# Perceiver block on one core: value projection for four heads at 512 columns, streamed value weights, and a reordered start of the tail

## What is computed

```
q = (query @ Wq + bq)            # 32 heads of 128, in 8 groups of 4
k, v = split(kv @ Wkv + bkv)     # 8 key/value heads of 128, kv = the 6272 context rows
scores = q.k / sqrt(128); attn = softmax(scores); o = attn @ v
x = x + o @ Wo + bo
```

## Time and profile before

| | us |
|---|---|
| median of 3 runs (1044.91 to 1045.31) | 1045.17 |
| the profiled execution | 1043.96 |
| its span, from the first to the last instruction | 1042.2 |
| PE busy | 1016.8 (98%) |
| DVE, ACT, POOL busy | 758.4, 590.3, 474.3 |

### The profile page before, as it was taken

How to read it: one execution, slowest core, us unless ns; L and a number is a source line. 1 busy time by engine, 2 the same in 40 slices (tenths; PEclk the granted TensorE clock), 3 DMA queues, 4 the chain that set the end, 5 groups by cost and what they waited for, 6 DMA issues and landing times.

```text
span 1042.2 us, 19683 instructions
## 1 busy us (share of the span) xinstructions
PE 1016.8 (98%) x7083; PEld 933.9 (90%) x7083; DVE 758.4 (73%) x1676; ACT 590.3 (57%) x1249; POOL 474.3 (46%) x637
## 2 busy tenths in 40 slices
PE   7999999999999999999999999999999999999997
PEld 5878989999999999999999999999999999999643
DVE  5777777767877687777876777777877678766665
ACT  5465566556656566555665566565665556655430
POOL 2344544455534545455544455445454444544330
PEclk9999999999999999999999999999999999999999
DMA  9731211122212222122221222112222115353966
GB/s 311 245 126 59 64 55 55 59 65 59 69 41 69 76 63 69 41 69 67 71 57 54 65 60 69 59 56 68 66 63 65 57 42 168 118 152 117 304 201 221
DMA packets 73537, 98.91 MB, mean 95 GB/s; under 512 B 8688, under 2 KB 42496, under 8 KB 73440
## 3 DMA queue, kind: packets, MB, share of 16 engines
q1 hardware_dynamic: 72448, 96.12, 30.1%
q10 hardware_dynamic: 896, 1.51, 0.4%
q0 software_dynamic: 96, 0.02, 0.0%
HBM read 82.81 MB, written 14.81 MB: 94 GB/s over the span
## 4 chain that ended last, share of the span: by engine, by line
PE 86%; DMA 5%; DVE 4%; ACT 2%; POOL 2%; SPq 1%; issue 1%; POOLq 0%; DVEq 0%
PE p_kv L73 18%; PE p_kv L74 18%; PE p_kv L75 18%; PE p_t L670 7%; PE p_o L73 4%; PE p_o L74 4%; PE p_o L75 4%; PE p_s L73 2%; PE p_s L74 2%; PE p_s L75 2%; PE p_s L753 2%; DMA wkv_raw<-in_wkv 1%; PE p_o L680 1%; PE p_ot L658 1%; DMA expanded_weights<-slots 1%; DMA ctx_st<-in_ctx_t 1%
## 5 line engine op out<-in xcount | busy, mean ns | idle before, releaser
L523 POOL TENSOR_SCALAR slots<-code 128x512 f32<-128x512 bf16 x232 | 154.1, 664 | 224.0 <-DVE slots L1296 153.3
L1292 DVE TENSOR_TENSOR slots<-slots 128x512 f32<-128x512 f32 x232 | 176.3, 760 | 3.3 <-POOL slots L523 1.5
L543 POOL TENSOR_TENSOR slots<-slots 128x512 f32<-128x512 f32 x58 | 75.7, 1304 | 202.5 <-DVE slots L1292 202.5
L1101 ACT ACTIVATE slots<-code,drop_and_offsets 128x512 f32<-128x512 bf16 x232 | 148.4, 714 | 29.8 <-POOL slots L543 29.1
L1245 DVE TENSOR_TENSOR v_lo<-p_kv,v_hi 128x256 fp32r<-128x256 f32 x196 | 83.2, 425 | 107.7 <-ACT v_hi L1066 106.6
L1066 ACT ACTIVATE v_hi<-p_kv 128x256 fp32r<-128x256 f32 x196 | 75.1, 384 | 137.8 <-PE p_kv L75 137.2
L1257 DVE TENSOR_TENSOR pt_lo<-p_t,pt_hi 128x512 fp32r<-128x512 f32 x224 | 133.4, 617 | 23.3 <-ACT pt_hi L1077 23.3
L1247 DVE SCALAR_TENSOR_TENSOR k_lo<-p_kv,bk_sb,k_hi 128x448 fp32r<-128x448 f32 x112 | 76.3, 682 | 100.3 <-ACT k_hi L1066 99.6
L1066 ACT ACTIVATE k_hi<-p_kv,bk_sb 128x448 fp32r<-128x448 f32 x112 | 70.9, 634 | 130.7 <-PE p_kv L75 129.8
L1077 ACT ACTIVATE pt_hi<-p_t 128x512 fp32r<-128x512 f32 x224 | 115.0, 542 | 41.6 <-PE p_t L670 41.5
L73 PE MATMUL p_kv<-wkv_hi,ctx_even_hi 128*128 128x256 f32 x448 | 126.4, 282 | 1.0 <-DVE v_lo L1245 0.9
(11 more groups left out here) (238 smaller groups left out, 2694.2 us busy)
## 6 DMA issues: line engine op xcount, KB each, us to landing
code<-in_codes SPq DMA_DIRECT2D x58, 256.0 KB, 2.7
scale<-in_scales SPq DMA_DIRECT2D x116, 128.0 KB, 3.1
expanded_weights<-slots SPq DMA_DIRECT2D x56, 256.0 KB, 2.1
ctx_st<-in_ctx_t SPq DMA_DIRECT2D x96, 112.0 KB, 2.0
ring_hi<-expanded_weights SPq DMA_DIRECT2D x22, 256.0 KB, 5.4
ring_lo<-expanded_weights SPq DMA_DIRECT2D x22, 256.0 KB, 5.3
wq_hi<-in_wq SPq DMA_DIRECT2D x4, 1024.0 KB, 6.5
wq_lo<-in_wq SPq DMA_DIRECT2D x4, 1024.0 KB, 6.5
```

Of the source, the lines that this page charges most:

```text
L523: nc.gpsimd.tensor_scalar(slots[:, slot, :], code16[:], LINES[j][0], LINES[j][1], ALU.mult, ALU.add).then_inc(pool_lines, 1)
L1101: nc.scalar.activation(slots[:, slot, :], code16[:], ACT.Identity, bias=offsets[:, k:k + 1], scale=LINES[j][0]).then_inc(act_lines, 1)
L1292: nc.vector.tensor_tensor(slots[:, slot, :], slots[:, slot, :], slots[:, other, :], ALU.max).then_inc(merged, 1)
```

## The change

- `values` runs only in blocks 0 and 4 of a chunk and projects four heads at once: 7 tiles of 12 matmuls of 512 columns. `v_hi`, `v_lo` hold four heads; splits and roundings have 512 columns.
- The value weights no longer stay. SP loads the 512 columns of the next group (1 MB) into `vw_lo` when the values of this one are done (`load_vw`); ACT and DVE round and split them in two halves of 128x1024, in the two blocks that follow (`round_vw`, `split_vw`). The key weights are loaded in four pieces.
- The NF4 tiles are no longer one to a block: of four tiles n to n+3, three are joined inside the block with the values and the fourth in the fourth block. Merges 0 to 4 of tile n stand ahead of the first split of values; those of n+1 and n+2 stand between the splits, by `between_tiles`. The context pieces are spread as `BLOCK_PIECES`.
- The ring has 18 slots, with a new `AHEAD`; SP's `scales_of(NB + 1)` is gone from its stream, POOL issues that load; the last blocks' attention turns, `fold(0)`, and the sums on DVE change their order.

In the rewritten schedules only the new side is shown, in the order SP, POOL, PE, ACT, DVE.

```diff
-PAIR_PIECES = (5, 5, 5, 1)
+VGROUP = 4
+VCOLS = VGROUP * D
+BLOCK_PIECES = (4, 2, 2, 2, 4, 1, 1, 0)
...
+        vw_hi = sb(st, "vw_hi", [P, KT, VCOLS], F32R)
+        vw_lo = sb(st, "vw_lo", [P, KT, VCOLS], F32R)
+        v_hi = sb(st, "v_hi", [P, CT, VCOLS], F32R)
+        v_lo = sb(st, "v_lo", [P, CT, VCOLS], F32R)
...
-        KV_USES = CT + 4
+        KV_USES = CT + 2 * VGROUP
+        GROUPS = NKV // VGROUP
...
+        RING_PLACES = [("hi", 0), ("lo", 0), ("hi", 1), ("lo", 1), ("hi", 2), ("lo", 2), ("v_hi", 0), ("v_hi", 1),
+                       ("v_lo", 0), ("v_lo", 1), ("hi", 3), ("lo", 3)]
+        WB = RING_ODD + len(RING_PLACES)
...
+            def load_vw(group):
+
+                if group >= 1:
+                    s, h = (group - 1) // GROUPS, (group - 1) % GROUPS * VGROUP
+                    sp.wait_ge(kv_psum, v_use(s, h, CT - 1) + 1)
+                first = NKV * D + group % GROUPS * VCOLS
+                sp.dma_start(vw_raw[:], wkv[:, :, first:first + VCOLS]).then_inc(vw_in, 16)
 
...
+                    if h % VGROUP == 0:
+                        if start:
+                            load_wq(3)
+                        load(0)
+                        codes_of(n + 2)
+                        if start:
+                            load_wq(4)
+                        load(1)
+                        if start:
+                            load_wq(5)
+                        tile_out(n)
+                        scales_of(n + 1)
+                        if start:
+                            load_wkv(2)
+                            load_wq(6)
+                        if last and h == 0:
+                            for dst, src in ((co, coefs), (mk, mask)):
+                                sp.dma_start(dst[:], src).then_inc(coef_in, 16)
                         codes_of(n + 3)
+                        load(2)
+                        tile_out(n + 1)
+                        scales_of(n + 2)
+                        if start:
+                            load_wq(7)
+                        codes_of(n + 4)
+                        load(3)
+                        if GROUPS * s + h // VGROUP + 1 < GROUPS * NCH:
+                            load_vw(GROUPS * s + h // VGROUP + 1)
+                        if start:
+                            load_wkv(3)
+                        tile_out(n + 2)
+                        scales_of(n + 3)
+                        if last:
+                            ring_slots(h)
+                    elif h % VGROUP == 1:
+                        load(0)
+                        codes_of(n + 5)
+                        load(1)
+                        if last:
+                            ring_slots(h)
...
-                if slot == WB + 12:
-                    scales_of(NB + 1)
...
+                    if h % VGROUP == 0:
+                        last_line(n)
+                        narrow(n + 1)
+                        split(0)
+                        join(n)
+                        first_lines(n + 1)
+                        add_rowsum(i, h)
+                        last_line(n + 1)
+                        narrow(n + 2)
+                        split(1)
+                        join(n + 1)
+                        first_lines(n + 2)
+                        last_line(n + 2)
+                        narrow(n + 3)
+                        split(2)
+                        join(n + 2)
+                        first_lines(n + 3)
+                        split(3)
+                    elif h % VGROUP == 1:
+                        last_line(n + 3)
+                        narrow(n + 4)
+                        split(0)
+                        add_rowsum(i, h)
+                        split(1)
+                    elif h % VGROUP == 2:
+                        split(0)
+                        add_rowsum(i, h)
+                        split(1)
+                    else:
+                        split(0)
+                        add_rowsum(i, h)
+                        if last and h == NKV - 1:
+                            wait_apart(pool, rows_in, 16 * len(rows), pool_passed)
+                            nc.gpsimd.tensor_tensor(x_bo[:], x_sb[:], bo_sb[:], ALU.add).then_inc(step("x_bo"), 1)
+                            nc.gpsimd.memset(la[:, :, 5 * RANK:6 * RANK], 0.0).then_inc(step("la_apart"), 1)
+                            nc.gpsimd.tensor_tensor(two_idents[:], ident[:, 0:TOK], ident[:, TOK:P], ALU.add).then_inc(
+                                step("two_idents"), 1)
+                        join(n + 3)
+                        first_lines(n + 4)
+                        split(1)
 
...
+            wait_apart(pool, scaled, NB + 1, pool_passed)
+            for b in range(2):
+                pool.dma_start(scale[b * QBLK:(b + 1) * QBLK, :],
+                               scales[NB + 1, b].partition_broadcast(QBLK)).then_inc(step("last_scale_in"), 16)
...
-                        m = split_matmuls(nc, p_kv[:, v_bank(h, t), 0:2 * D], ctx_hi[half][:, k, keys],
-                                          ctx_lo[half][:, k, keys], wkv_hi[:, k, cols], wkv_lo[:, k, cols],
+                        m = split_matmuls(nc, p_kv[:, v_bank(h, t)], ctx_hi[half][:, k, keys],
+                                          ctx_lo[half][:, k, keys], vw_hi[:, k], vw_lo[:, k],
...
-            prev_values(NCH, 0)
-            turn_attention(5)
-            project_out(5)
-            turn_attention(6)
-            turn_output(NB - 1)
-            project_out(6)
-            turn_attention(7)
-            project_out(7)
-            used[0] += 3 * KT // 2
...
+            turn_attention(5)
+            turn_attention(6)
+            prev_values(NCH, 0)
+            project_out(5, 0)
+            turn_output(NB - 1)
+            project_out(5, 1)
+            project_out(6)
+            turn_attention(7)
...
             pe.wait_ge(step("two_idents"), 1)
             mean_and_turn(0, xa)
...
+            def round_vw(n):
+                act.wait_ge(vw_in, 16 * (n // 2 + 1))
+                nc.scalar.activation(vw_piece(vw_hi, n), vw_piece(vw_raw, n), ACT.Copy).then_inc(vw_rounded, 1)
...
+                if h % VGROUP == 0:
+                    for t in range(CT):
+                        if i == 0 and t in (1, 2, 4, 5):
+                            query_out({1: 2, 2: 3, 4: 4, 5: 5}[t])
                         round_values(s, h, t)
+                        if t == 0:
                             round_ctx(s, h, half, 0, last)
+                        elif t == 1:
+                            lines(n + 1, part=slice(0, 2))
+                        elif t == 2:
+                            lines(n + 1, part=slice(2, 4))
+                        elif t == 3:
+                            round_ctx(s, h, half, 1, last)
+                            if s == 0:
+                                round_wkv(h // 2 + 1)
+                        elif t == 4:
+                            lines(n + 2, part=slice(0, 2))
+                        elif t == 5:
+                            lines(n + 2, part=slice(2, 4))
+                        else:
+                            round_ctx(s, h, half, 2, last)
                     if i == 0:
+                        query_out(6)
...
+                    group = GROUPS * s + h // VGROUP + 1
+                    if h % VGROUP < 3 and group < GROUPS * NCH:
+                        round_vw(2 * group + h % VGROUP - 1)
+                    round_ctx(s, h, half, 0, last)
...
+                if h % VGROUP == 0:
+                    lines(n + 3)
+                elif h % VGROUP == VGROUP - 1:
+                    lines(n + 4)
...
+            def split_vw(n):
+                dve.wait_ge(vw_rounded, n + 1)
+                nc.vector.tensor_tensor(vw_piece(vw_lo, n), vw_piece(vw_raw, n), vw_piece(vw_hi, n).bitcast(F32),
+                                        ALU.subtract).then_inc(vw_split, 1)
...
+                if h % VGROUP == 0:
+                    for k in range(5):
+                        merge(n, k)
+                    between_tiles = {0: ((0, 5),), 1: ((1, 0),), 2: ((1, 1), (1, 2), (1, 3)), 3: ((1, 4), (1, 5)),
+                                     4: ((2, 0),), 5: ((2, 1), (2, 2), (2, 3)), 6: ((2, 4), (2, 5))}
                     for t in range(CT):
+                        if i == 0 and t in (1, 2, 4, 5):
+                            finish_query({1: 1, 2: 2, 4: 3, 5: 4}[t])
+                        split_kv(v_use(s, h, t), v_lo[:, t], p_kv[:, v_bank(h, t)], v_hi[:, t])
+                        for later, k in between_tiles[t]:
+                            merge(n + later, k)
+                        if s == 0 and t == 3:
+                            split_wkv(h // 2 + 1)
+                    if i == 0:
+                        finish_query(5)
                 else:
...
+                    for k in range(2):
+                        merge(n + 3, 2 * (h % VGROUP - 1) + k)
+                    if s == 0 and h == 2:
+                        split_wkv(2)
```

(3 more changed lines are left out.)

300 lines of the change are left out of this document (111 added, 189 removed).

## The result

The changed kernel takes **1076.78 us** (median of 4 runs, 1076.01 to 1077.85), the kernel before on the same chip 1045.24 (1044.91 to 1045.70). The ratio is 1.030, with a 95% interval of 1.028 to 1.031: slower by 31.5 us. The prediction named 1065.0, with a range of 1037 to 1080 and 0.70 on slower.

The account below looks back on a forecast made before the run. PE bounds the kernel before; after, the NF4 chain beside the values. 1043.96 + 20.0 (chain) - 0.5 (first group) + 1.7 (start) + 1.2 (second group) - 2.6 (tail) = 1063.8, named 1065.0 since runs' median lay 1.2 higher; range 1037 to 1080.

Parts of the forecast that it names:

- What decides: First block of a group: three NF4 tiles' merges delay value splits, PE waits, each four-block group grows by 1.54 us.
- M0: End of merge 5 of the group's first NF4 tile, put at 10.3 us after the block's first score matmul.
- M1: End of merge 5 of the group's second NF4 tile, put at M0+10.2 = 20.5 us.
- Start: Before the first score: the first value weights, 1 MB instead of 0.5 MB, cost 1.7 us, bounds 0 and 3.4.
- Chunk 0: First group gains 0.5 us because query products give the chain time; second loses 1.54 plus 1.2 for a key-weight split.
- Matmul time: Value projections: 512-column matmuls at 230.9 ns each, bounds 213.8 and 236.7; gain 6.8 us if PE stays the bound.
- The rival at 214 to 216 ns: PE stays the bound with 214 to 216 ns per 512-column matmul: gain 24 us, time 1020, chance 5%.
- Streaming: Each group's 1 MB value-weight load, roundings and splits stay hidden from PE; without DVE's cover 1.2 us in 26 blocks.
- Tail: After the last block: SP's scaling wait goes, PE's slot waits with it, 2.6 us saved; bounds -5 and +3.
- PE-bound: Rival: PE stays the bound with faster 512-column matmuls, split 6 ending before 27.4; 1037.5 us, chance 17%.
- tie: Rival: the NF4 chain runs at its lower bound; 1046 us, chance 8%.
- The heavier case: Rival: 1 MB load delays the third tile's write by 3.4 us, 1 us more in 13 groups; 1078 us, chance 12%.

Follow-up runs that it names:

- e3: Changed kernel with two NF4 tiles beside the values instead of three, merges placed between splits where their inputs are ready: 1045.42 us, ratio 1.0022.
- e6: e3 with the first block's fourth context load ahead of the tile's write, and six ring loads instead of four ahead in the last block: 1025.69 us, ratio 0.981.
- e1: Changed kernel with ACT's lines for the next NF4 tile ahead of the second context piece in a group's fourth block: 1068.47 us, ratio 1.024.
- e4: Kernel before, with only the last NF4 tile's scales issued by POOL instead of SP: 1041.85 us, ratio 0.9983.
- e7: e1 with the join's product in an eighth slot, so POOL's third line need not wait for the tile's write: 1057.85 us, ratio 1.012.
- e2: Changed kernel without the 1 MB value-weight loads after the first; roundings and splits stay, later values come from wrong weights: 1075.68 us, ratio 1.031.
- e10: e6 with the next group's value weights rounded and split one block later, in the third and fourth block: 1029.16 us, ratio 0.987.
- the eighth slot: Join's product in its own slot, sparing POOL's third line the wait for the write: 1057.85 us added to e1, 1026.32 us added to e6.

## Why the prediction was right, and where it was off

**What decides: held.** The chain of three NF4 tiles beside the values sets the first block; PE's own speed does not enter. The three waits of PE stand where the text put them: expected 0.4, 0.95 and 0.65 us, measured in block 24 0.36, 1.12 and 0.76 (in block 16, of an even chunk, 0.18, 1.01 and 0.69). e3 bears it out: the same 512-column matmuls with one tile fewer beside them, and the merges placed anew, leave no idle time in the block. And blocks 24 and 32 of the kernel after are equally long, 33.70 and 33.74 us, though where PE is the bound (e6) the second of them takes 0.46 us more. The busy share of a steady chunk is 133.94 of 138.76, 96.5%, under the 98% that the text named.

**Length of the chain: mis-sized by 0.7 us a group.** M0 was put at 10.3 and measured 10.28. The round was put at 10.2 and was 10.64, because merges 4 and 5 took 1.85 us and not 1.3: POOL's narrow and its context split run beside them. From M1 to the end of split 6 it was 9.19 instead of 8.9. The upper bound held both sums, though not the single term (1.7 us for the last two merges, where 1.85 were measured). So block 24 was 33.70 us and not 33.0.

**The step that failed: "three tiles must pass inside one block" was worked out as if every such block began alike.** The merges were put at 4.91 into the block, from block 23. ACT's queue ahead of that, where the lines of the next group's first tile were moved behind a context rounding, was not followed back to SP's queue. At h = 4 it makes merges start at 6.20 (block 20) and the block 35.4 us long, 6 to 7 us in all (e1). The prediction said of ACT only that it is not late in its rounding and takes its lines in pairs. The order on both queues could be read from the changed kernel; the length of the wait, 3.45 us, is in no row of before.

**Start.** The first score came 0.65 us later, not 1.7. The chain of waits of the kernel after, its first 25 us, has this load in it (columns as in the earlier trace rows):

```profile
3.60 12.89 DMA vw_raw<-in_wkv
```

The 1 MB load took 12.89 us where 512 KB had taken 12.17. In that stretch the queues move 307 to 318 GB/s in either kernel, so the extra 0.5 MB seems to have taken the place of other loads and not to have come on top of them; no run varies this load alone. Kernels with the 1 MB load had the first score at 20.17 to 20.83, those with the old one at 19.55 and 20.11 (e4 and before), so 0.65 is hardly more than the spread.

**Chunk 0: sign wrong.** The first group was to give 0.5 us and cost 2.2. "The query products give the chain its time" left out that the tile's write shares the queue with their weights: POOL waits 5.26 us for it in block 0, and with that wait taken out of the way (e7) the block is 6.2 us shorter than in e1. The second group cost 1.6 where 1.5 and 1.2 were named.

**Matmul time: the mean right, the reading from one chunk.** With 128-column weights in a stream that nothing interrupts, the price depends on the chunk. The values of e6 in blocks 16 and 24 (first matmul of values, first of keys), and those of a block of before in chunk 3:

```profile
304.72 0.39 PE L75 MATMUL p_kv<-vw_hi,ctx_even_hi 128*128 128x512 f32 x1
...
324.31 0.36 PE L75 MATMUL p_kv<-ctx_even_hi,wkv_hi 128*128 128x448 f32 x1
...
436.56 0.40 PE L75 MATMUL p_kv<-vw_hi,ctx_odd_hi 128*128 128x512 f32 x1
...
455.62 0.36 PE L75 MATMUL p_kv<-ctx_odd_hi,wkv_hi 128*128 128x448 f32 x1
```

```profile
446.35 0.28 PE L73 MATMUL p_kv<-wkv_hi,ctx_odd_hi 128*128 128x256 f32 x1
...
456.43 0.36 PE L73 MATMUL p_kv<-ctx_odd_hi,wkv_hi 128*128 128x448 f32 x1
```

84 matmuls of 512 columns take 19.59 us in an even chunk and 19.06 in an odd one, 233 and 227 ns each; 84 of 256 columns take 9.94 and 10.08. From block 8 on every stretch of values without a wait, in before and in e6, agrees with the one of its chunk's kind to 0.02 us. So a group gains 0.29 us in an even chunk and 1.1 in an odd one. With 8 groups in even chunks and 6 in odd ones the mean price is 230.5 ns, where the prediction assumed 230.9, and the gain if PE is the bound is 8.9 us, not the forecast 6.8: the earlier trace rows are of an even chunk, where two matmuls of 256 columns are cheapest. Why the chunks differ, which read different context buffers, no run shows. e6, where PE is the bound, has 781.05 us for blocks 8 to 54 against 788.72 before, 7.7 less, with idle time of 1.2 and 1.4 us in it (before has 1.1 and 0.9). The rival at 214 to 216 ns falls. The Trainium skill's single gap (TensorE: Matmul & The Clock Gate, Back-to-back issue gap) gives 216 ns; the trace does not agree, by 11 to 17 ns in each matmul, all with 128-column weights loaded for each. The 11 us for the matmuls in the expectation of e3 took the odd chunk's 227 and the even chunk's 118.3, and are too high by 2.

**Streaming: right for this kernel** (e2). With PE as the bound it does show in a few second blocks: in e6's block 9 ACT waits 1.8 us for the load and PE 1.2. And the 1.2 us that the prediction said would show if the cover on DVE went points the same way as e10's loss in its fourth block, which came to 0.3 to 0.55 us a group. **Tail: nearly right,** -3.6 for -2.6. No wait of PE for a ring slot is left, SP's 11.8 us is gone, and e4 shows 2.5 of it to be the scales alone. The other 1.1 may be the new order of turns and folds, put at zero with bounds of 1 each way; that was not tried by itself.

**The rivals.** PE-bound and tie did not come about with the order as changed, but a kernel at the PE bound exists, e6, with another order. It ran 12 us under this rival's 1037.5. The largest part is chunk 0, which the rival left as it was: 146.9 us in e6 from the first score to block 8 and 153.9 before; which of the changes gives that was not tried. The heavier case comes nearest to the measured time, with 1078, by a mechanism that e2 refutes. That the measured 1076.8 lies inside the range, and just inside the forecast's own of 1052 to 1077, is in part luck. Blocks 8 to 54 grew by 13.2 us more than forecast, and about half of that is ScalarE's wait (6.5 us there in e1), which stands in no bound of the working: the room that took it in had been left for slow merges and for the heavier case.

## What to carry to other kernels

When work is packed beside a faster operation, lay out the slower engines' chain in time before the faster one's gain is counted; here 31.5 us were lost, most of them to a chain for which there was room one block later, and 1025.7 us were to be had with the same matmuls. Of the 18.1 us by which e6's span is under that of before, blocks 8 to 54 give 7.7, chunk 0 7.1 and the tail 3.4. Follow every wait that a moved instruction now stands behind, through the queue that issues its load: the same pattern, a transfer that an engine awaits standing behind another on one queue, cost 6 to 7 us in the kernel after (a load behind a write), 12 us of idle in e3 (the same) and 6 in block 0 (a write behind a load). The worth of an edit belongs to the path it lies on: the eighth slot gave 10.6 us in one kernel and nothing in the other. And a price read in one place is checked in a second: here it differs between even and odd chunks by as much as the gain that was reckoned from it.

## What the hardware showed that was not expected

A 256 KB write issued 0.6 us behind a 1 MB load on the same queue landed 6.7 us after its issue at 36.09, where the median is 2.1. That fits what the Trainium skill says (DMA: Bandwidth & Descriptors, Queues, rings and completion order), that on each DMA engine descriptors are consumed in ring order; whether the write would be as late on the other queue was not tried.

DVE's merges, with both inputs in SBUF, take 0.6 us from start to start alone and up to 1.03 beside POOL in the kernel after, while splits that read PSUM keep their 0.6: in block 24, 473.83 to 474.85 for a merge and 474.85 to 475.45 for the split behind it, with POOL's line and then its cast beside them. The Trainium skill (SBUF — State Buffer, Who interferes with whom) has DVE and GpSimd share one port pair under an exclusive lock, for which a DVE instruction with two SBUF inputs contends with a GpSimd one that reads SBUF, and one with at most one input there, outside the 2-port modes, does not. The trace agrees in which of the two is slowed; whether one waits for the whole of the other's instruction is left open.

A matmul of 512 columns costs 233 ns in even chunks and 227 in odd ones, while one of 256 columns costs 118 and 120, at the same granted clock and with the same instructions on another context buffer.
